# A decoder layer in one kernel: the last residual folded into the base weights, its layer norm read from PSUM, and a shorter routing step

## The reference, cut to what matters

```python
x = _layernorm(x + mamba_block_and_mlp(x))        # LN1
x = _layernorm(x + softmax(x @ ctx.T) @ ctx)      # LN2
# the third one, x2 being LN2's output:
logits = x2 @ gate_w.T + expert_bias              # 4 experts
one_hot = jax.nn.one_hot(jnp.argmax(logits, -1), 4)
z = jnp.einsum('nh,erh->ner', x2, lora_A)         # rank 8 for each expert
delta = jnp.einsum('neh,ne->nh', jnp.einsum('ner,ehr->neh', z, lora_B), one_hot)
x = _layernorm(x2 + x2 @ W_up.T + delta)          # LN3
```

## Time and profile before

| what | value |
|---|---|
| median of 3 executions | 395.36 us |
| the profiled execution | 395.69 us |
| its span on the core | 393.9 us |
| PE, DVE, ACT, POOL busy | 97%, 72%, 49%, 39% of the span |
| granted clock of TensorE over the span | 0.995 |
| chain that ended last: PE, DVE, POOL, ACT | 67%, 16%, 6%, 4% |

### The profile page before, as it was taken

One profiled execution on the slowest core, in us unless ns is written; L12 is line 12 of the kernel. 1 busy time (PEld: TensorE's weight loads), 2 busy tenths in 40 slices (PEclk: granted clock), 3 DMA queues, 4 the chain that ended last, 5 costly groups with the idle time before them and its releaser, 6 DMA issues.

```text
span 393.9 us, 5382 instructions
## 1 busy us (share of the span) xinstructions
PE 381.2 (97%) x1923; PEld 309.8 (79%) x1927; DVE 284.2 (72%) x501; ACT 193.0 (49%) x390; POOL 152.8 (39%) x139
## 2 busy tenths in 40 slices
PE   8999998999999999999999999999999999999983
PEld 3878886766688998888888888878788888897862
DVE  5599891267764987979797979695666756676575
ACT  7868767866757544242424243863314144142241
POOL 6407325944499732838283837850000000000000
PEclk9999999999999999999999999999999999999998
DMA  8901110110001033120212111451110120101002
GB/s 272 317 3 54 55 53 6 48 55 0 2 0 55 1 114 121 36 99 20 94 33 75 56 53 53 140 175 59 55 54 28 54 82 27 53 27 53 27 2 81
DMA packets 11659, 25.52 MB, mean 65 GB/s; under 512 B 1681, under 2 KB 1809, under 8 KB 11634
## 3 DMA queue, kind: packets, MB, share of 16 engines
q1 hardware_dynamic: 10480, 23.10, 17.8%
q10 hardware_dynamic: 1154, 2.10, 1.4%
HBM read 23.10 MB, written 2.10 MB: 64 GB/s over the span
## 4 chain that ended last, share of the span: by engine, by line
PE 67%; DVE 16%; POOL 6%; ACT 4%; issue 4%; DMA 2%; SPq 0%; DVEq 0%; ACTq 0%
PE bank_first L655 8%; PE bank_first L657 8%; PE bank_first L656 8%; PE bank L655 7%; PE bank L657 7%; PE bank L656 6%; DVE big L1533 5%; PE bank_last L655 5%; PE bank_last L657 5%; PE bank_last L656 5%; PE bank L924 2%; POOL rows L544 2%; PE bank L935 2%; DMA raw<-wstream 2%; DVE sets L1670 1%
## 5 line engine op out<-in xcount | busy, mean ns | idle before, releaser
L655 PE MATMUL bank_first<-sets,station 128*128 128x512 f32 (+1 forms) x172 | 69.9, 406 | 0.1
L655 PE MATMUL bank<-sets,station 128*128 128x512 f32 (+1 forms) x180 | 67.2, 373 | 1.1 <-POOL station L491 0.6
L656 PE MATMUL bank<-sets,station 128*128 128x512 f32 (+1 forms) x180 | 65.8, 366 | 0.0
L657 PE MATMUL bank<-sets,station 128*128 128x512 f32 (+1 forms) x180 | 65.8, 366 | 0.0
L657 PE MATMUL bank_first<-sets,station 128*128 128x512 f32 (+1 forms) x172 | 65.6, 381 | 0.0
L656 PE MATMUL bank_first<-sets,station 128*128 128x512 f32 (+1 forms) x172 | 65.4, 380 | 0.0
L655 PEld LDWEIGHTS bank<-sets,station 128*128 128x128 f32 x180 | 33.9, 188 | 7.8 <-POOL station L487 1.0
L655 PEld LDWEIGHTS bank_first<-sets,station 128*128 128x128 f32 x172 | 32.5, 189 | 8.4 <-issue 2.8
L656 PEld LDWEIGHTS bank<-sets,station 128*128 128x128 f32 x180 | 34.0, 189 | 5.9 <-issue 0.5
L657 PEld LDWEIGHTS bank<-sets,station 128*128 128x128 f32 x180 | 34.0, 189 | 5.5
L656 PEld LDWEIGHTS bank_first<-sets,station 128*128 128x128 f32 x172 | 32.4, 189 | 6.8 <-issue 1.7
(11 more groups left out here) (247 smaller groups left out, 864.2 us busy)
## 6 DMA issues: line engine op xcount, KB each, us to landing
raw<-wstream SPq DMA_DIRECT2D x31, 512.0 KB, 3.6
rows<-x SPq DMA_DIRECT2D x8, 256.0 KB, 4.7
big<-ctxT SPq DMA_DIRECT2D x8, 256.0 KB, 2.7
big<-ctx SPq DMA_DIRECT2D x8, 256.0 KB, 3.0
out<-tmp ACTq DMA_DIRECT2D x8, 256.0 KB, 2.0
big<-ln_w SPq DMA_DIRECT2D x1, 256.0 KB, 5.0
big<-lora_b SPq DMA_DIRECT2D x3, 64.0 KB, 4.8
ga<-gate_lora SPq DMA_DIRECT2D x1, 72.0 KB, 4.9
```

The lines of the kernel that those rows point to most:

```text
L655: pe.matmul(ps, a_hi, b_lo, start=first, stop=False)
L656: pe.matmul(ps, a_hi, b_hi, start=False, stop=False)
L657: return pe.matmul(ps, a_lo, b_hi, start=False, stop=last)
```

## The change

1. POOL, behind its last work, adds the 128x128 identity to the four diagonal blocks of W_up.T in `raw` (x2 @ (W + I) is x2 @ W + x2), and counts `eye_ok`; ACT's `bw_high` waits for two adds for each chunk.
2. `add_ffn` goes. LN3's moments (`ffn_moments`) and scaling (`ffn_normed`) read the PSUM pair directly; the wait for an earlier store moves from the addition to the scaling.
3. `base` waits for the previous tile's scaling (`ln_out[2]`) where it waited for its addition (`ln_u[2]`).
4. In `routed` the comparison (L1800) and the product (L1804) become one `scalar_tensor_tensor`, 128x32, which reads PSUM.
5. `bw_low(0)` and `bw_low(1)` move from ahead of DVE's step 1 to behind `normed(0)` in it.
6. At the end by hand, `ffn_normed(5)` stands behind `low_halves(7)`, the moments of tile 6 behind `route(7)`, and both of the last scalings at the end.

```diff
+            for c in range(DC):
+                n = base_load(c // 2)
+                pool.wait_ge(raw_in[raw_slot(n)], landed(n))
+                diagonal = raw[:, raw_slot(n), bass.ds((c % 2) * D + c * P, P)]
+                pool.tensor_tensor(diagonal, diagonal, ident[:, :], ALU.add).then_inc(eye_ok, 1)
...
-                        pe.wait_ge(ln_u[2], t if free is None else free)
+                        pe.wait_ge(ln_out[2], t if free is None else free)
...
                 act.wait_ge(raw_in[raw_slot(n)], landed(n))
+                act.wait_ge(eye_ok, 2 * (i + 1))
                 act.activation(baseS[:, 0, bass.ts(i, 2), 0:D], in_two(raw[:, raw_slot(n), :]), ACT.Copy).then_inc(bw_hi, 1)
...
+            def ffn_moments(t, pair=6, slot=None):
+                k = 2 if slot is None else slot
+                v.wait_ge(ffn_ps, t + 1)
+                v.bn_stats(stats[:, k, :], pair_of[pair][:, :, 0:D // 2]).then_inc(ln_st[2], 1)
+                v.wait_ge(ln_st[2], t + 1)
+                v.bn_aggr(mv[:, k, :], stats[:, k, :]).then_inc(ln_mv[2], 1)
+
+            def ffn_normed(t, u=u3, pair=6, slot=None, stored_tiles=None):
+                if stored_tiles is not None:
+                    v.wait_ge(stored, 16 * stored_tiles)
+                normed(2, t, in_two(u), slot, src=pair_of[pair][:, :, 0:D // 2])
...
-                v.tensor_scalar(u, u, mv[:, k, 0:1], lrs[:, k:k + 1], ALU.subtract, ALU.mult).then_inc(ln_out[i], 1)
+                v.tensor_scalar(u, u if src is None else src, mv[:, k, 0:1], lrs[:, k:k + 1], ALU.subtract, ALU.mult).then_inc(ln_out[i], 1)
...
-                v.tensor_scalar(lg[:, 2, :], lg[:, 1, :], gm[:, 1:2], None, ALU.is_equal).then_inc(lg_step, 1)
-                v.wait_ge(lg_step, 5 * t + 5)
...
-                v.tensor_tensor(z.rearrange("p (e r) -> p e r", e=E),
-                                bank[bk][:, D // 2 + E:D // 2 + E + er].rearrange("p (e r) -> p e r", e=E),
-                                lg[:, 2, :].unsqueeze(2).broadcast_to([P, E, RANK]), ALU.mult).then_inc(z_step, 1)
+                v.scalar_tensor_tensor(out=z.rearrange("p (e r) -> p e r", e=E),
+                                       in0=lg[:, 1, :].unsqueeze(2).broadcast_to([P, E, RANK]), scalar=gm[:, 1:2],
+                                       in1=bank[bk][:, D // 2 + E:D // 2 + E + er].rearrange("p (e r) -> p e r", e=E),
+                                       op0=ALU.is_equal, op1=ALU.mult).then_inc(z_step, 1)
...
-            def add_ffn(t, par, u=u3, pair=6, stored_tiles=None):
-                v.wait_ge(ffn_ps, t + 1)
-                if stored_tiles is not None:
-                    v.wait_ge(stored, 16 * stored_tiles)
-                v.tensor_tensor(in_two(u), pair_of[pair][:, :, 0:D // 2], in_two(u2[:, par, :]), ALU.add) \
-                    .then_inc(ln_u[2], 1)
...
                 if g:
-                    add_ffn(t - 3, 1 - par, stored_tiles=None if first_g else t - 3)
-                    moments(2, t - 3, u3)
+                    ffn_moments(t - 3)
                 if a:
                     normed(0, t - 1, u1)
+                if base_weights:
+                    bw_low(0)
+                    bw_low(1)
                 if g:
-                    normed(2, t - 3, u3)
+                    ffn_normed(t - 3, stored_tiles=None if first_g else t - 3)
...
             tail(0, 0, a=False, f=False, g=False)
-            bw_low(0)
-            bw_low(1)
-            tail(1, 1, f=False, g=False)
+            tail(1, 1, f=False, g=False, base_weights=True)
...
             low_x2(last - 1)
-            add_ffn(last - 2, 1, stored_tiles=last - 2)
-            moments(2, last - 2, u3)
+            ffn_moments(last - 2)
             add_attention(last, 1)
             moments(1, last, u2[:, 1, :])
             choose(last - 1, bk=1)
             normed(1, last, u2[:, 1, :])
             routed(last - 1, bk=1)
             low_halves(last)
-            add_ffn(last - 1, 0, u=u1, pair=0)
-            normed(2, last - 2, u3)
+            ffn_normed(last - 2, stored_tiles=last - 2)
             route(last)
-            moments(2, last - 1, u1)
-            add_ffn(last, 1, u=u_last)
-            moments(2, last, u_last, slot=0)
-            normed(2, last - 1, u1)
-            normed(2, last, u_last, slot=0)
+            ffn_moments(last - 1, pair=0)
+            ffn_moments(last, slot=0)
+            ffn_normed(last - 1, u=u1, pair=0)
+            ffn_normed(last, u=u_last, slot=0)
```

More of the change, by code:

```diff
@@ L300, in build @@
         hid_hi, hid_lo, down_ps = sem("hid_hi"), sem("hid_lo"), sem("down_ps")
-        ln_u, ln_st, ln_mv, ln_log, ln_rs, ln_out = (
-            [sem(f"ln{i}_{what}") for i in (1, 2, 3)] for what in ("u", "st", "mv", "log", "rs", "out"))
+        eye_ok = sem("eye_ok")
+        ln_u = [sem(f"ln{i}_u") for i in (1, 2)]
+        ln_st, ln_mv, ln_log, ln_rs, ln_out = (
+            [sem(f"ln{i}_{what}") for i in (1, 2, 3)] for what in ("st", "mv", "log", "rs", "out"))
         q_ps, q_ok, sc_ps, mx_ok, ex_ok = sem("q_ps"), sem("q_ok"), sem("sc_ps"), sem("mx_ok"), sem("ex_ok")
@@ L1778, in moments, with normed @@
                 v.bn_aggr(mv[:, k, :], stats[:, k, :]).then_inc(ln_mv[i], 1)
-            def normed(i, t, u, slot=None):
+            def ffn_moments(t, pair=6, slot=None):
[8 more added lines that the diff above has]
+                normed(2, t, in_two(u), slot, src=pair_of[pair][:, :, 0:D // 2])
+            def normed(i, t, u, slot=None, src=None):
                 k = i if slot is None else slot
                 v.wait_ge(ln_rs[i], t + 1)
-                v.tensor_scalar(u, u, mv[:, k, 0:1], lrs[:, k:k + 1], ALU.subtract, ALU.mult).then_inc(ln_out[i], 1)
+                v.tensor_scalar(u, u if src is None else src, mv[:, k, 0:1], lrs[:, k:k + 1], ALU.subtract, ALU.mult).then_inc(ln_out[i], 1)
             def choose(t, bk=7):
@@ L1788, in choose @@
                 v.tensor_tensor(lg[:, 0, :], bank[bk][:, D // 2:D // 2 + E], eb[:, :], ALU.add).then_inc(lg_step, 1)
-                v.wait_ge(lg_step, 5 * t + 1)
+                v.wait_ge(lg_step, 4 * t + 1)
                 v.tensor_reduce(gm[:, 0:1], lg[:, 0, :], AX.X, ALU.max).then_inc(lg_step, 1)
-                v.wait_ge(lg_step, 5 * t + 2)
+                v.wait_ge(lg_step, 4 * t + 2)
                 v.scalar_tensor_tensor(out=lg[:, 1, :], in0=lg[:, 0, :], scalar=gm[:, 0:1], in1=codes[:, :],
@@ L1795, in routed @@
             def routed(t, bk=7):
-                v.wait_ge(lg_step, 5 * t + 3)
+                v.wait_ge(lg_step, 4 * t + 3)
                 v.tensor_reduce(gm[:, 1:2], lg[:, 1, :], AX.X, ALU.max).then_inc(lg_step, 1)
-                v.wait_ge(lg_step, 5 * t + 4)
-                v.tensor_scalar(lg[:, 2, :], lg[:, 1, :], gm[:, 1:2], None, ALU.is_equal).then_inc(lg_step, 1)
-                v.wait_ge(lg_step, 5 * t + 5)
+                v.wait_ge(lg_step, 4 * t + 4)
                 er = E * RANK
                 z = zm[:, 3 * er:4 * er]
-                v.tensor_tensor(z.rearrange("p (e r) -> p e r", e=E),
-                                bank[bk][:, D // 2 + E:D // 2 + E + er].rearrange("p (e r) -> p e r", e=E),
-                                lg[:, 2, :].unsqueeze(2).broadcast_to([P, E, RANK]), ALU.mult).then_inc(z_step, 1)
+                v.scalar_tensor_tensor(out=z.rearrange("p (e r) -> p e r", e=E),
+                                       in0=lg[:, 1, :].unsqueeze(2).broadcast_to([P, E, RANK]), scalar=gm[:, 1:2],
+                                       in1=bank[bk][:, D // 2 + E:D // 2 + E + er].rearrange("p (e r) -> p e r", e=E),
+                                       op0=ALU.is_equal, op1=ALU.mult).then_inc(z_step, 1)
                 v.wait_ge(z_step, 2 * t + 1)
@@ L1854, in add_attention, with tail @@
                                        op0=ALU.mult, op1=ALU.add).then_inc(ln_u[1], 1)
-            def tail(t, par, a=True, f=True, g=True, split=True, first_g=False):
+            def tail(t, par, a=True, f=True, g=True, split=True, first_g=False, base_weights=False):
                 if a:
@@ L1894, in _ @@
             moments(0, last - 1, u1)
-            add_ffn(last - 3, 0, stored_tiles=last - 3)
-            moments(2, last - 3, u3)
+            ffn_moments(last - 3)
             normed(0, last - 1, u1)
-            normed(2, last - 3, u3)
+            ffn_normed(last - 3, stored_tiles=last - 3)
             low_x2(last - 2)
```

## The result

The kernel after took 397.09, 397.51, 397.55 and 395.89 us, median 397.3, beside 395.41 for the kernel before on the same chip: ratio 1.0037 [1.0022, 1.0053], some 1.5 us slower. (The ratio is that of the means, 397.01 and 395.52; the brackets hold it with 95%.) The forecast was +0.6 us. The ratio puts the time at 396.9, the upper end of the range. At +0.37% it is also just beyond the 0.3% that the prediction called "the same": the likeliest case came out too low, and the side it had given a chance of 0.11 is the better name for the result. That is the key to it.

What follows compares the result with a forecast made beforehand. PE bounds the steady steps, DVE the start up to 267 us, and a chain of waits through all engines the end. Start +0.54 and end +0.06 make +0.60 on the median 395.36: 396.0 us, range 394.9 to 396.9.

Steps and rivals of the forecast that it cites:

- Start +0.54: Tile 1's start: two POOL additions each delay DVE by 0.27 us ahead of `hid_lo`, so `down(1)` begins 0.54 later.
- Rival A: Start: POOL's additions fall into gaps or come second, nothing lost; only the end counts, 395.4 us; chance 0.18.
- rival B: Start: port holds `hid_lo` for all four additions at full length, 1.86 us; total 397.3 us; chance 0.11.
- C: End: last addition comes off in full, with twice 0.21 in routing, -1.14 us, so 394.2; chance 0.05.
- D: Scaling from PSUM no dearer than from SBUF and no loss at the start: -0.43, 394.9 us; chance 0.08.
- ACT's wait: Start: ACT's `bw_high` waits for POOL's additions; `rstd` of tile 0 waits 0.4 us, costing nothing.
- `bw_low` later gains nothing: DVE, first steps: the base weights' low parts, 2.35 us, move into idle time; what this unblocks was in time already.
- Scaling from PSUM: LN3's scaling on DVE: 0.75 us taken, between 0.54 and 0.81, for 0.52 to 0.55 from SBUF.
- `base(7)` waits for the scaling, +1.02: End: tile 5's scaling stands behind `low_halves(7)` on DVE, so `base(7)` begins at 384.24 for 383.22, 1.02 us later.
- Routing -0.21: `routed` on DVE: two instructions become one, saving 0.21 us a tile, which counts only for tile 7.
- Sum of the end +0.06: Last tiles: the last scaling ends at 391.50 for 391.44, +0.06 us; from -0.43 to +0.34 with prices low or high.
- The list of signs: Expected in the profile after: POOL's additions, stretched DVE rows, `down(1)` at 267.6, `base(7)` held, last scaling 6.8 to 7.5 us behind it.

Runs made afterwards that it cites:

- e5: Kernel after, with POOL's four additions held until `split_hid(1)` is done and ACT's high parts put behind the first `rstd`: ratio 1.0039 to the kernel before.
- e6: Kernel before plus only POOL's identity additions and ACT's wait for them (later x2 addition left in): median 397.06 us, ratio 1.0040.
- e8: Kernel after, unedited, timed again on another occasion: 11 executions, median 396.25 us, ratio 1.0024 to the kernel before.
- e1: Kernel after, unedited, timed again: five executions from 396.36 to 397.33 us, ratio 1.0040 to the kernel before.
- e2: Kernel after plus five useless matmuls on PE in the gap ahead of the last `base`: median 395.94 us, ratio 1.0011 to the kernel before.
- e3: Kernel after, with tile 5's scaling moved ahead of `low_halves(7)` and one more chunk of `base(7)` ahead of `lora(6)`: median 394.94 us, ratio 0.9979.
- e4: Kernel after, with only tile 5's scaling moved, to behind `normed(1, 7)` on DVE: median 395.50 us, ratio 0.9998 to the kernel before.
- e9: The kernel of e5 timed again, on one chip with e8: 12 executions, median 396.81 us, ratio 1.0028 to the kernel before.

## Why the prediction was right or wrong

- **PE bound in the steady steps, DVE at the start: right.** PE was busy in all 95.63 of 95.63 us after, and `down(1)` still waited for L1770.
- **Start +0.54: right in mechanism and size.** +0.53 by the trace, two steps of 0.27, and e5 took it away. Rival A (nothing lost) falls. So does rival B: 397.3 was its number and is the median measured, but its mechanism, a port that holds `hid_lo` for four additions, is not in the trace. A right number is no proof of its story. (Its 4 x 0.46 is 1.84, not 1.86, which changes nothing.) C and D fall with the wait of `base(7)` and the dearer scaling.
- **ACT's wait: nothing, right**; PE has no new wait in the steady steps.
- **"`bw_low` later gains nothing": wrong.** Set against the kernel before it may be so (no run moves the splits without the additions), but the additions make the base splits late, and e6 shows 1.16 us lost at `turn_x1(0)` when DVE's splits stay in front. The step costed the two parts separately, while one part pays for the other. The sum was not hurt, since both were made.
- **Scaling from PSUM: 0.75 taken, 0.78 to 0.80 measured**, for 0.52 to 0.55 from SBUF. The upper bound of 0.81 was nearer. The Trainium skill ("VectorE: DVE Perf Modes", section "Why PSUM operands drop a tier") would have given it: the trace agrees. The moments took 0.70 from PSUM for 0.69: as forecast.
- **`base(7)` waits for the scaling, +1.02: right**, 1.07. Its wait of 1.38 us is the longest of PE in the kernel after.
- **Routing -0.21: right.** L1825 takes 0.25 with its extra scalar, and the routing of tile 7 lasts 1.54 us for 1.74.
- **Sum of the end +0.06: this is the step that failed.** It priced the new wait as a delay alone. In 11 of 20 executions the time is that of the lower clock, with which the matmuls up to the routing took 1.42 us longer. With the share of each set (3/4, 4/5, 4/11) of the 1.24 between the groups, and the forecast's 0.6, the three sets would come to 1.5, 1.6 and 1.05 us; the ratios 1.0037, 1.0040 and 1.0024 are 1.5, 1.6 and 0.95. (The shares are read off the same executions, so this accounts for the times and forecasts nothing.) Without that term the forecast was right: the lower group of e8 is at +0.59, and the one such execution in each of the other sets at +0.48 and +0.83.
- **The list of signs** named no granted clock. One of its signs failed for that reason: the last scaling ends 8.78 us behind `base(7)` in the profile after, not 6.8 to 7.5 (7.29 in e1, where the clock held). Another missed slightly: `base(7)` starts 0.87 behind `low_halves(7)`, not 0.7 to 0.8. The earlier trace rows had a hint: 0.93 from 382 to 391.5 us. That was the time after 390 us, where PE has nothing left to do. It shows that the clock can fall once PE is idle in this stretch, and the forecast put a new idle time there.

Of the fall itself, only part is explained. Shown: it needs the idle time of PE (e2, which fills it, and e3 and e4, which shorten it, have no execution above 396.6), and the lower clock makes the difference in time. Not shown: why the same 1.38 us brings it down in one execution and not in the next. The end of the traces varies in the same way: before, the clock fell some 1.6 us after PE's last matmul (388.62 to about 390.2), in e1 some 3.9 us after it (389.70 to about 393.6). The Trainium skill ("TensorE: Matmul & The Clock Gate", section "Part 1: The HAM clock gate (the "warmup" mystery)") says that the activity is looked at in windows that run free of the program, so that one kernel can show different counts of slow matmuls. The two groups fit that; no run here tests it.

## What to carry to other kernels

A wait moved onto TensorE near the end, where it has little work in reserve, costs its length and may also cost the clock of the matmuls behind it: look at the granted clock around every idle stretch of PE before pricing a new one. Before a result is judged by its operations, try the places: the same operations were 0.2 to 0.4% slower than before or 0.1 to 0.2% faster by where one scaling of 0.8 us and one block of matmuls stood. And look at single times, not the median alone, when four of them lie in two groups: an edit is then compared group with group, as e9 with e8.

## What was not expected of the hardware

- After an idle time of 1.38 us, PE ran at a granted clock of 0.50 from about 384.0 to 387.4 us, although it was busy all the while, and in another execution of the same kernel, after the same 1.38 us, at 1.00. Waits of 0.71 (e3) and 0.86 (e4) left it at 1.00 in the profiles taken.
- With POOL's 128x128 addition beside it, DVE's split lost 0.27 for 0.43 of POOL's time: less than the whole length, as in the earlier trace rows with the 128x256 ones. The Trainium skill ("SBUF — State Buffer", section "SBUF: two separate sides") has the lock last for the full instruction, which would cost 0.43 by the length that e5 shows (an estimate): the trace shows less. POOL pays more than DVE: its four additions took 5.46 us in all, 1.44 each in the median, for 1.72 in all without DVE's two-input work.
